# Narrow attention on column strips, with the softmax shift inside ScalarE's exponential

## The reference

```python
# layer 0, cross attention (stage "b"): 32 heads of width 16, keys and values from ctx (16, 128, 256)
q, (k, v) = rope(x @ Wq), split(ctx @ Wkv);  k = rope(k)
w = softmax(q k^T / sqrt(16));  x = layernorm(x + (w v) @ Wout + bout)
# layer 1, self attention (stage "d"): 16 heads of width 32, attending over the first axis with a causal mask
w = softmax(mask(q k^T / sqrt(32)));  x = layernorm(x + (w v) @ Wo)
```

## Time and profile before

| | |
|---|---|
| median of 3 runs | 3754.5 us (3750.48 to 3756.18) |
| profiled execution | 3771.24 us, span of its instructions 3769.4 us |
| mean granted TensorE clock | 0.926 |
| TensorE matmuls busy | 3284.9 us, 87% of the span |
| VectorE / ScalarE / GpSimd busy | 54% / 32% / 38% |
| stage b | from about 980 to 1495 us of the span |
| stage d | from about 2070 to 2455 us |

### The profile page before, as it was taken

The page is one execution under the profiler, slowest core; times in us unless marked ns, Lnnn a source line. Parts: engine busy times, 40 slices in busy tenths (PEclk is TensorE's granted clock), DMA queues, the critical chain, the costliest instruction groups (busy, mean ns, idle before and its releaser), DMA issues. The chain is left out here.

```text
span 3769.4 us, 56030 instructions
## 1 busy us (share of the span) xinstructions
PE 3284.9 (87%) x19560; PEld 2766.9 (73%) x19560; DVE 2045.0 (54%) x3614; ACT 1215.3 (32%) x2825; POOL 1424.5 (38%) x1452
## 2 busy tenths in 40 slices
PE   7999999999699998349987899979999999739992
PEld 5878878888588887237765688758888888529892
DVE  4676575666456553401117455456767677425556
ACT  2333333333334443000110333234444444214440
POOL 3554343444211111240026222145555566255455
PEclk9999999999789997668999899989999999869996
DMA  4000040111100001402957211141101000056664
GB/s 159 17 28 34 0 130 12 44 44 61 69 19 28 21 21 45 159 3 82 340 180 169 71 36 36 34 137 33 45 11 45 11 23 11 3 188 232 236 236 150
DMA packets 129137, 301.90 MB, mean 80 GB/s; under 512 B 18602, under 2 KB 30634, under 8 KB 126467
## 3 DMA queue, kind: packets, MB, share of 16 engines
q1 hardware_dynamic: 111938, 263.14, 20.6%
q0 software_dynamic: 15360, 36.25, 3.7%
q10 hardware_dynamic: 1728, 1.07, 0.1%
HBM read 236.90 MB, written 77.60 MB: 83 GB/s over the span
## 5 line engine op out<-in xcount | busy, mean ns | idle before, releaser
L377 POOL TENSOR_TENSOR a_sq<-a_tq,a_sinq 128x256 f32<-128x256 f32 x128 | 150.1, 1191 | 356.8 <-DVE a_tq L448 356.8
L377 POOL TENSOR_TENSOR a_sk<-a_tk,a_sink 128x256 f32<-128x256 f32 x128 | 123.7, 986 | 90.0 <-DVE a_tk L448 90.0
L1609 POOL DMA_INDIRECT packed<-moe_xall,moe_rows x96 | 93.7, 977 | 158.2 <-issue 158.2
L1040 DVE TENSOR_REDUCE b_nmax<-bank 128x8 f32<-128x1024 f32 x64 | 78.4, 1224 | 138.4 <-PE bank L1169 138.3
L941 POOL TENSOR_TENSOR d_prob<-d_prob,d_nmax 128x1024 f32<-128x1024 f32 x32 | 60.9, 1904 | 232.2 <-DVE d_nmax L1038 232.2
L1190 PEld LDWEIGHTS bank<-b_va,b_probT 128*128 128x128 f32 x1024 | 140.4, 203 | 11.1 <-ACT b_probT L856 2.9
L390 POOL TENSOR_TENSOR e_sk<-e_tk 128x512 f32<-128x512 f32 x64 | 66.6, 1040 | 210.9 <-DVE e_tk L475 210.9
L343 ACT COPY a_probT<-bank 128x512 f32<-128x512 f32 x64 | 37.5, 586 | 328.5 <-PE bank L653 328.5
L335 ACT ACTIVATE e_prob<-bank,e_nb,e_rq 128x128 f32<-128x128 f32 x256 | 113.8, 455 | 83.5 <-DVE e_nb L540 83.5
L330 ACT ACTIVATE a_sm<-a_sm,a_nmax 128x128 f32<-128x128 f32 x256 | 99.8, 391 | 122.3 <-DVE a_nmax L535 122.3
L1190 PE MATMUL bank<-b_va,b_probT 128*128 128x17 f32 x1024 | 131.5, 262 | 2.0 <-ACT b_probT L856 2.0
(11 more groups left out here) (498 smaller groups left out, 10817.9 us busy)
## 6 DMA issues: line engine op xcount, KB each, us to landing
n_wg<-in_f_wg SPq DMA_DIRECT2D x24, 704.0 KB, 4.5
n_wu<-in_f_wu SPq DMA_DIRECT2D x24, 704.0 KB
cw_wg<-in_c_wg SPq DMA_DIRECT2D x32, 512.0 KB
cw_wu<-in_c_wu SPq DMA_DIRECT2D x32, 512.0 KB
cw_wd<-in_c_wd SPq DMA_DIRECT2D x32, 512.0 KB
packed<-all_zero SPq DMA_DIRECT2D x32, 384.0 KB, 4.1
n_xe<-packed SPq DMA_DIRECT2D x48, 256.0 KB
n_wd<-in_f_wd SPq DMA_DIRECT2D x24, 512.0 KB, 6.6
```

The source lines that it names most:

```text
L377: step = nc.gpsimd.tensor_tensor(o, i, s, ALU.mult)
L1040: nc.vector.tensor_reduce(nmax[:, p], scores, AX.X, ALU.max, negate=True).then_inc(v_nm, 1)
L1609: nc.gpsimd.indirect_dma_start(packed, bass.IndirectOffsetOnAxis(ap=rows[:, b, k:k + 1], axis=0), xall[:, b, :], None, bounds_check=bound, ...
```

## The change

- `probs_v` now takes two slots (8 heads) at once, every other slot. The values, 32 columns of a head, are stationary, and the 128 columns of the transposed probabilities move. Head j of a slot writes 32 PSUM partitions from 32j on: a column strip of the array of its own. In b a head fills 16 of the 32 columns and the other 16 are zero, and two heads accumulate into one strip. A second set of matmuls with `ones` stationary puts the sum of the exponentials, repeated over the partitions, beside the result.
- The result has the features on the partitions, so `turn_z` is gone; ScalarE rounds z from SBUF. `take_z` takes a reciprocal of 128x256 and multiplies 128x256, per half. The rows of the output weights are permuted on the host to fit.
- In b (not in d) VectorE scales the negated maximum by 1/sqrt(16) into `nb` (128x8), and ScalarE exponentiates head by head from `pS` with `nb` as bias: 8 instructions of 128x128. The next `scores` wait for these.
- x is transposed into `pJ` in place of `pT`, at the head of slot 0, and waits for the copy of v out of `pJ`; the waits of the q and k rounds for z are gone. The plans are reordered.

```diff
-        va = st.sbuf("va", [P, 2, NH, DH + 1])
+        va = st.sbuf("va", [P, 2, NH, W])
+        ones = st.sbuf("ones", [P, SUBS, W])
...
             def take_z(b):
-                act.wait_ge(pe_zt, done(b))
+                for n in range(2):
+                    act.wait_ge(v_z[n], done(b))
                 act.wait_ge(pe_o, done(b - 1))
-                nc.scalar.copy(z_hi[:], pT[:, :]).then_inc(act_zt, 1)
+                nc.scalar.copy(z_hi[:], zn[:]).then_inc(act_zt, 1)
...
+                act.wait_ge(pe_pt, done(2 * w - 3))
+                for i in range(2 * H):
+                    step = nc.scalar.activation(prob[:, p % 2, i], pS[:, i // H, P * (i % H):P * (i % H) + P], ACT.Exp,
+                                                bias=nb[:, p % 2, i:i + 1], scale=SCALE)
+                step.then_inc(act_e, 1)
...
             def slot(b, s, par, back=True, ahead=True, older=True):
                 u = UN * b + s
+                if s == 0 and ahead:
+                    take_x(b + 1)
...
             def take_z(b, n):
                 dve.wait_ge(pe_z[n], done(b))
-                dve.wait_ge(pe_zt, done(b - 1))
-                z = pZ[n][:, 0:HB * (DH + 1)].rearrange("p (h d) -> p h d", h=HB)
-                nc.vector.reciprocal(rinv[:, n], z[:, :, DH]).then_inc(v_r[n], 1)
+                nc.vector.reciprocal(rT[:, n], pZ[n][:, 2 * P:4 * P]).then_inc(v_r[n], 1)
...
-                    dve.wait_ge(pe_pt, done(u - 3))
-                    nc.vector.tensor_tensor(prob[:, p], scores, nb, ALU.add).then_inc(v_low, 1)
+                    dve.wait_ge(act_e, done(w - 2))
+                    nc.vector.tensor_scalar(nb[:, p], nmax[:, p], SCALE, None, ALU.mult).then_inc(v_low, 1)
...
             def turn_x(b):
                 pe.wait_ge(x_in, landed(b))
-                pe.wait_ge(act_t, done(2 * ROUNDS * b - 1))
+                pe.wait_ge(act_v, done(b - 1))
...
             def turn(b, n):
-                pe.wait_ge(v_xl, done(b))
-                pe.wait_ge(v_zl, done(b - 2 if n >= TURNS_BEFORE_Z else b - 3))
...
             def scores(w, s, par):
-                pe.wait_ge(v_sm if causal else v_low, done(w - 1))
+                pe.wait_ge(v_sm if causal else act_e, done(w - 1))
...
             def probs_v(u, b, s, par):
+                pe.wait_ge(act_pt, done(u + 1))
+                n = 2 * s // UN
+                if s % (UN // 2) == 0:
+                    pe.wait_ge(v_z[n], done(b - 1))
+                for sums in (False, True):
+                    for i in range(2):
+                        blk, sub = (s + i) % (UN // 2) // SUBS, (s + i) % SUBS
+                        col = 2 * P * sums + P * blk
+                        for j in range(H):
+                            left = ones[:, sub] if sums else va[:, par, place(s + i, j)[0]]
+                            last = nc.tensor.matmul(pZ[n][W * j:W * j + W, col:col + P], left, probT[:, s // 2 % 2, i, j, :],
+                                                    start=sub == 0, stop=sub == SUBS - 1)
...
 PLAN_8
     "pe": [
-        ["s", "p", ("o2", 8, 12), "pv", "x"],
+        ["x", "s", "p", ("o2", 8, 12)],
         ["p", ("q", 0, 3), "pv"],
-        ["s", "p", ("q", 3, 9), "pv"],
-        ["p", ("q", 9, 12), "pv", ("k", 0, 3)],
-        ["s", "p", ("k", 3, 6), "pv", "zt"],
+        ["s", "p", ("q", 3, 9)],
+        ["p", ("q", 9, 12), "pv"],
+        ["s", "p", ("k", 0, 6)],
         ["p", ("v", 0, 3), "pv", ("v", 3, 6), 0],
-        ["s", "p", 1, "pv", ("o", 0, 4), 2],
-        ["p", "pv", 3, ("o", 4, 8)],
+        ["s", "p", ("o", 0, 2), 1, ("o", 2, 4), 2],
+        ["p", ("o", 4, 6), 3, ("o", 6, 8), "pv"],
     ],
-    "dve": [["s", "x", "z0"], ["y"], ["s", "n"], ["q"], ["z1", "s", "k"], ["zt"], ["s"], []],
-    "act": [["x", "c"], [], [], [], [], ["zt", "v", 0], [1, 2], [3]],
+    "dve": [["x", "s", "z0"], ["y"], ["s", "n"], ["q"], ["z1", "s", "k"], ["zt"], ["s"], []],
+    "act": [["c"], [], [], [], ["zt"], ["v", 0], [1, 2], [3]],
 PLAN_4
     "pe": [
-        ["s", "p", ("o2", 0, 6), "x", "pv", ("o2", 6, 12)],
-        ["p", ("q", 0, 6), "pv", ("q", 6, 12)],
+        ["x", "s", "p", ("o2", 0, 6), "pv", ("o2", 6, 12)],
+        ["p", ("q", 0, 12)],
         ["s", "p", ("k", 0, 6), "pv", 0, ("k", 6, 12)],
-        ["p", "zt", ("v", 0, 6), "pv", 1, ("v", 6, 12)],
+        ["p", ("v", 0, 6), 1, ("v", 6, 12)],
     ],
-    "dve": [["s", "x", "z0"], ["y"], ["s", "q", "n", "z1"], ["k", "zt"]],
-    "act": [["x"], [], [0], ["zt", 1, "v"]],
+    "dve": [["x", "s", "z0"], ["y", "q"], ["s", "n", "z1"], ["k", "zt"]],
+    "act": [[], [], [0], ["zt", 1, "v"]],
```

More of the change, by code:

```diff
@@ L688, in narrow_attention @@
     LAG = plan["lag"]
-    in_order = [e for slot in plan["pe"] for e in slot if e == "zt" or isinstance(e, int)]
-    TURNS_BEFORE_Z = in_order.index("zt")
+    SUBS = W // DH
     with ExitStack() as ctx:
@@ L757, in narrow_attention @@
         n_const = 16 * (3 if rope else 1)
+        n_made = 3 + SUBS * SUBS + (2 if rope else 0)
         block = ctx.enter_context(nc.Block())
@@ L825, in take_x @@
                     act.wait_ge(pe_v, done(b - 1))
-                nc.scalar.copy(x_hi[:], pT[:, :]).then_inc(act_x, 1)
+                nc.scalar.copy(x_hi[:], pJ[:, :]).then_inc(act_x, 1)
             def take_context(b):
@@ L845, in take_v @@
                 act.wait_ge(pe_z1, done(b - 2))
-                nc.scalar.copy(va[:, par, :, 0:DH], heads(pJ[:, :], NH)).then_inc(act_v, 1)
+                if SUBS == 1:
+                    nc.scalar.copy(va[:, par], heads(pJ[:, :], NH)).then_inc(act_v, 1)
+                    return
+                quarters = va[:, par].rearrange("p (g t) w -> p g (t w)", t=2).rearrange("p g (f d) -> p g f d", d=DH)
+                nc.scalar.copy(quarters[:, :, 0:4:3, :], heads(pJ[:, :], NH).rearrange("p (g t) d -> p g t d", t=2)).then_inc(act_v, 1)
             def take_t(b, par, n):
@@ L901, in _ @@
             nc.gpsimd.memset(mhalf[:], -0.5).then_inc(g_c, 1)
-            nc.gpsimd.memset(va[:], 1.0).then_inc(g_c, 1)
+            nc.gpsimd.memset(va[:], 0.0).then_inc(g_c, 1)
+            for t in range(SUBS):
+                for r in range(SUBS):
+                    nc.gpsimd.memset(ones[:, t, DH * r:DH * r + DH], 1.0 if r == t else 0.0).then_inc(g_c, 1)
             nc.gpsimd.memset(eps[:], EPS).then_inc(g_c, 1)
@@ L906, in _ @@
                 nc.gpsimd.memset(ks[:], 0.0).then_inc(g_c, 1)
-            pool.wait_ge(g_c, 5 if rope else 3)
+            pool.wait_ge(g_c, n_made)
             pool.wait_ge(c_in, n_const)
@@ L1181, in probs_v @@
             def probs_v(u, b, s, par):
[L1182 removed]
+                pe.wait_ge(act_pt, done(u + 1))
                 if s == 0:
                     pe.wait_ge(act_v, done(b))
[L1185 to L1202 removed]
+                n = 2 * s // UN
[9 more added lines that the diff above has]
+                                                    start=sub == 0, stop=sub == SUBS - 1)
+                if s + 2 in (UN // 2, UN):
+                    last.then_inc(pe_z[n], 1)
             def output(b, parts, ahead=True):
@@ L1220, in slot @@
                         turn_prob(u - LAG, (s - LAG) % UN)
-                    if what == "pv" and (back or s >= LAG + 1):
-                        s1 = (s - LAG - 1) % UN
-                        here = s >= LAG + 1
-                        probs_v(u - LAG - 1, b if here else b - 1, s1, par if here else 1 - par)
+                    if what == "pv" and (back or s >= LAG + 2):
+                        here = s >= LAG + 2
+                        probs_v(u - LAG - 2, b if here else b - 1, (s - LAG - 2) % UN, par if here else 1 - par)
                     if ahead:
@@ L1235, in slot @@
                             turn(b + 1, what)
-                    if back and what == "zt":
-                        turn_z(b - 1, ahead)
                     if back and what == "o":
@@ L2405, in layout_l1_attn @@
         "d_wq": by_chunk(w[:D].T), "d_wk": by_chunk(w[D:2 * D].T), "d_wv": by_chunk(w[2 * D:].T),
-        "d_wo": by_chunk(i["L1_attn_weight_out"].T), "d_mask": np.where(seen, 0.0, NEG).astype(np.float32),
+        "d_wo": by_chunk(in_slots(i["L1_attn_weight_out"].T, 16)), "d_mask": np.where(seen, 0.0, NEG).astype(np.float32),
     }
```

71 lines of the change are left out of this document (28 added, 43 removed).

## The result

The kernel with the change takes 3663.7 us (median of 4 runs) beside 3752.5 us for the kernel before (4 runs of the same session): a ratio of 0.977, with an interval of 0.974 to 0.979. It is faster by 89 us. The prediction was 3753 us, no change, with a range down to 3722 us; the time lies outside it, near the 3680 us of rival 3.

The account below looks back on a forecast made before the run. TensorE was taken as the bound in both stages. Terms summed to -15 us in b, +9 us in d and +4 us at stage ends, together -2 us: a median of 3753 us from 3754.5, range 3722 to 3795 us.

Parts of the forecast that it names:

- rival 3: New "pv": all four strips stay busy, 0.028 us a record; ScalarE then bounds b near 25 us: about 3680 us, chance 0.06.
- The rate of a record: New "pv" on TensorE: two strips run at a time as in `scores`, 0.062 us a record, 2.07 us a pair.
- +1.25 and +0.41: TensorE's own work, "pv" and "zt" together: +1.25 us a batch in b, +0.41 us in d.
- the rest of the sum: Waits: b -1.15, -0.85, -0.43, +0.2 us a batch; d -0.64, +0.84; stage ends +4 us in all.
- weight loads hide only under another row group: New "pv": by this rule some 0.027 us of load is added to each record: 3830 us, chance 0.02.
- the case that the prediction called likeliest: New "pv" with two strips at a time: 3753 us, range 3738 to 3774 us, chance 0.70.
- +0.2 us: Stage b, slots 6 and 7 to slot 0: ScalarE's copies come late for `scores`, +0.2 us a batch.
- The wait for x and the clock: Stage b: x ahead of `scores` removes a wait, -1.15 us a batch, and the half-speed stretch behind it, -0.85 us.
- d's waits: Stage d: the wait for q's copy goes, -0.64 us a batch; a wait for v's copy comes, +0.84 us.
- ScalarE's chain: Stage b: `scores` to last exponential takes 5.4 us, hidden under 5.6 us of TensorE's work in slots 0 and 1.
- Hidden: VectorE: its work, with reciprocals of 1.75 us, falls to about 15.5 of 28 us in b, off the path.
- rival 2: Stage b: ScalarE's chain sets the pace, 0.5 to 1.2 us a batch more: 3761 to 3771 us, chance 0.12.

Follow-up runs that it names:

- e1: Changed kernel with probs_v's head loops turned round, so four records in a row go to one column strip: 3665.3 us, ratio 0.978 to the kernel before.
- e2: Changed kernel with the heads of a slot written to two column strips in place of four, same records: 3726.5 us, ratio 0.994 to the kernel before.
- e3: Changed kernel with all heads of a slot written to one column strip, same records: 3891.7 us, ratio 1.039 to the kernel before.
- e4: Kernel before with only stage b's turn of x moved to the head of slot 0 on all three engines: 3726.2 us, ratio 0.994.
- e10: Changed kernel with stage b's turn of x put back to the end of slot 0: 3606.6 us, ratio 0.982 to the kernel before.
- e8: Changed kernel with each 128x256 reciprocal in take_z done twice, first into a spare buffer: 3645.1 us, ratio 0.993 to the kernel before.
- e7: Changed kernel with stage d's turn of x moved behind the first half of o2 in slot 0: 3571.0 us, ratio 0.974 to the kernel before.
- e5: Changed kernel with stage b's old softmax (VectorE subtracts into SBUF, one exponential): 3580.7 us, ratio 0.976 to the kernel before.
- e11: Changed kernel with stage d's x turned later and stage b's old softmax: 3576.0 us, ratio 0.974 to the kernel before.
- e6: Kernel before with only stage b's new softmax (eight exponentials from PSUM, next scores wait for them): 3710.8 us, ratio 1.012.
- e9: Changed kernel with stage d's x turned later and, in b, the last k round copied before the probabilities: 3577.0 us, ratio 0.975 to the kernel before.

## Why the prediction was wrong, point by point

**The rate of a record is the step that failed.** It read "the second record of one head and the first of the next run together", from `scores`, and took 0.062 us. The record takes 0.028 us, and e1 shows that the order is indifferent: with four records of a strip in a row the time is the same. e2 and e3 show what counts, the number of strips. The row for `scores` had been read rightly (0.058 us) and carried over wrongly: it has two strips, and two column strips cost 0.056. A closer look at the same group of before shows it. The records that overlap 0.20 us from its start, and those within the first 0.04 us of the new "pv":

```profile
1201.40:1201.60 0.20, 0.20 (x2) 1.00 0.00 0
```

```profile
1152.19:1152.23 0.04, 0.03 (x4) 1.00 0.00 0
```

Two start together with two strips, four with four. With 1.10 us a pair the step gives 4 x (1.10 - 1.64) - 0.47 = -2.6 us a batch in b and 2 x (1.10 - 1.64) - 0.45 = -1.5 in d, in place of +1.25 and +0.41: 15 x (3.9 + 1.9) = 87 us lower. That alone would have given 3666 us for the 3664 measured. That it lands so near is luck: 17 us of the strips' gain came back as waits (e2), and the rest of the sum was too high by about as much (below). How records of one strip queue up while those of others run is not in the trace; that each strip has a queue of its own fits e1, and is only argued.

The Trainium skill ("TensorE: Matmul & The Clock Gate", Part 3) gives 2.38 for three column strips. The estimate by it was 26 us lower than my sum; the measured factor is 3.8 for four strips (0.111 to 0.029 us), and three were not run. The same part of the Trainium skill has the rule that weight loads hide only under another row group, which would have added to each record. This trace doesn't agree: with a load of 32 columns ahead of every record, the 0.111 us of one strip are about a quarter of the 0.43 us that the router's 512 columns take, so next to nothing of the load shows, on one strip either.

**With two strips the rest of the sum is about 20 us too high.** e2 is the case that the prediction called likeliest; it takes 21 us less than before, for a sum of -2. Some 10 us of it are the group itself (1.87 + 0.09 for 2.07 us, 96 groups). In the rest, the exponentials were shorter (2.18 for 2.65 us), and e2 has no wait of `scores` in b, where +0.2 us was counted, 3 us; what remains was not told apart.

**The wait for x and the clock.** e4 gains 22 us and e10 loses 21 to 24, for 30 predicted (1.15 + 0.85 us a batch). The size of the wait was right: 8.0 to 9.0 us of idle time in eight or nine batches wherever it stands, 1.2 us a batch by e4. The clock's 0.85 us was read rightly from one execution, the profiled one, and 22 us leave about 0.3 us a batch for it. That the clock falls because of the wait was not shown: e10 has the wait and a clock of 1.00, e8 has no such wait and 0.95.

**d's waits.** Right: q's wait gone, v's wait 0.93 us for 0.84, and worth 11 us by e7.

**ScalarE's chain.** That eight exponentials fit under TensorE's work in slots 0 to 3 can't be read from this kernel: the faster "pv" shortened that work by about 1 us a pair, to 5.07 and 5.24 us, and two short waits came of it (0.3 us for the exponentials, 0.4 us for k). Rival 3's "near 25 us a batch" came out as 24.5, but not for its reason: its own terms add up to 22.6 us, TensorE is busy for 97% of b, and it waits for ScalarE for only 0.8 us a batch. The 0.256 us from one exponential to the next (2.18 less 0.386, over 7) is below the 0.34 that was taken from stage e. By the Trainium skill ("ScalarE: Activation LUTs", "What ACT_TABLE_LOAD costs") eight take 2.4 us, an estimate; the trace has 2.18.

**VectorE is not covered by its low load.** "Hidden" was right for one reciprocal of 1.75 us and is wrong for a second (e8), though VectorE is busy for only 63% in b: in slot 2 its list had no slack left, the maximum was 0.16 us late already.

**The softmax edit is worth nothing in itself** (e5, e11), and rival 2 is what it does without the new order (e6). The prediction counted +0.2 us a batch for the new waits on it, 3 us. The two comparisons give 1 us for the old form and 2 us for the new one, so a term of this size can't be told from none.

The ledger, by ratios: two strips in place of the old form, with all other edits, -21 us; the second pair of strips -66 us; together the 87 of the 89 us that were measured. Inside the first figure stand -22 us for x ahead of `scores` and +11 to 13 us for d's wait for v.

## What to carry to other kernels

Count how many strips of the array a group of small matmuls fills: its rate goes with that number, and the trace shows the number as the records that start together in the group's first 40 ns. Moving an operand so that four strips are filled can pay even where each record moves more columns (128 for 17 here), and part of what it gives can come back as waits for the engine that feeds the next group: here 17 of 83 us, with ScalarE's copies and exponentials. When a wait is moved away, look up in the new trace what the next one ends on before naming it: in e9 and e10 it wasn't the queue that seemed near at hand. Judge an addition to an engine's list by what stands behind it until the next instruction of the bound engine, not by the share of time in which that engine is busy.

## What the runs showed of the hardware

- Column strips scaled without loss: 0.111, 0.056 and 0.029 us a record of 128 moving fp32 columns with one, two and four strips, each record with a weight load of 32 columns ahead of it; the order of the strips did not matter (e1, by its time).
- Eight exponentials of 128x128 from PSUM, each with its own bias, took 2.18 us: 386 ns each, 256 ns apart.
- The clock did not fall behind a wait of 1.0 us a batch in e10 (1.00 over ten batches), and did in about every second batch of the profiled execution of the kernel before (0.97) with the same wait. One such stretch made a batch 1.5 us longer.
- A VectorE instruction of 128x8 took 0.73 us when a GpSimd addition of 128x256 started 0.03 us ahead of it (e9), and 0.17 us when the addition came after it.
- The same kernel took 3747 us on one chip and 3670 us on others. The stage between the router's logits and the experts took about 224 us on the one and about 150 us on the others; it lies outside the change.
